# Causal masks of attention from TensorE to VectorE, and softmax maxima from matmuls to DMA, in a fused scan, attention and experts kernel

## The reference, cut to what matters

```python
t = t + attn(ln_t(t), Wk, Wq, Wv, Wu, bu)     # t: 8 images x 1024 tokens x 128
# inside attn, 8 heads of 128:
dot = einsum('bhqe,bhke->bhqk', queries, keys) / sqrt(e)
dot = where(tril(ones(t, t)), dot, -inf)
attn = softmax(dot, axis=-1)
out = einsum('bhqk,bhke->bqhe', attn, values).reshape(b, t, h * e)
return out @ Wu.T + bu
```

## Time and profile before

| | |
|---|---|
| median of 3 runs | 2596.7 us (2596.37 to 2597.08) |
| profiled execution, its own time | 2594.88 us |
| its span, first to last instruction | 2593.1 us |
| PE busy | 2389.7 us (92%) |
| DVE busy | 1641.9 us (63%) |
| POOL busy | 1636.7 us (63%) |
| ACT busy | 1359.5 us (52%) |
| mean granted TensorE clock | 0.921 |

### The profile page before, as it was taken

One profiled execution on the slowest core, in us unless ns is written; L12 is line 12 of the kernel. 1 busy time (PEld: TensorE's weight loads), 2 busy tenths in 40 slices (PEclk: granted clock), 3 DMA queues, 4 the chain that ended last, 5 costly groups with the idle time before them and its releaser, 6 DMA issues. The chain is left out here.

```text
span 2593.1 us, 45062 instructions
## 1 busy us (share of the span) xinstructions
PE 2389.7 (92%) x14307; PEld 1954.7 (75%) x14307; DVE 1641.9 (63%) x3626; ACT 1359.5 (52%) x3319; POOL 1636.7 (63%) x1773
## 2 busy tenths in 40 slices
PE   4798999999996999999999999999999999399994
PEld 2577777777774888888888888888888887288883
DVE  5777877787545566666666666667666664244444
ACT  3655565655532566666566656665666655133331
POOL 3678877887741556576676675766756758255551
PEclk9987887887786999999999999999999999599996
DMA  3920000000000000010010010100100100255555
GB/s 103 386 97 2 9 9 1 9 1 1 17 1 25 1 1 23 2 32 9 3 36 3 8 33 2 33 8 4 36 2 9 33 1 32 79 195 194 196 187 196
DMA packets 61693, 130.97 MB, mean 51 GB/s; under 512 B 9157, under 2 KB 27631, under 8 KB 61462
## 3 DMA queue, kind: packets, MB, share of 16 engines
q1 hardware_dynamic: 51222, 106.82, 12.1%
q0 software_dynamic: 9088, 17.07, 1.9%
q10 hardware_dynamic: 1152, 4.19, 0.4%
HBM read 64.78 MB, written 65.10 MB: 50 GB/s over the span
## 5 line engine op out<-in xcount | busy, mean ns | idle before, releaser
L1135 POOL TENSOR_TENSOR plo<-pf,phi 128x512 fp32r<-128x512 f32 (+3 forms) x768 | 775.8, 1014 | 478.4 <-ACT phi L1374 403.7
L1372 ACT ACTIVATE pf<-psum 128x512 f32<-128x512 f32 (+3 forms) x768 | 378.0, 492 | 498.0 <-PE psum L1274 343.9
L1515 DVE TENSOR_REDUCE peak<-psum 128x1 f32<-128x512 f32 (+3 forms) x512 | 302.9, 592 | 229.2 <-PE psum L1245 121.6
L1374 ACT ACTIVATE phi<-psum 128x512 fp32r<-128x512 f32 (+3 forms) x768 | 374.5, 488 | 0.0
L1245 PE MATMUL psum<-xT,qT 128*128 128x512 f32 (+3 forms) x768 | 304.1, 396 | 10.8 <-DVE nmax L1509 5.2
L1194 PE MATMUL psum<-phi,x_tok 128*128 128x512 f32 (+3 forms) x768 | 307.5, 400 | 0.0
L1194 PE MATMUL psum<-qT,xT 128*128 128x512 f32 (+3 forms) x768 | 266.8, 347 | 0.0
L1196 PE MATMUL psum<-phi,x_tok 128*128 128x512 f32 (+3 forms) x768 | 265.9, 346 | 0.0
L1196 PE MATMUL psum<-qT,xT 128*128 128x512 f32 (+3 forms) x768 | 265.7, 346 | 0.0
L1195 PE MATMUL psum<-qT,xT 128*128 128x512 f32 (+3 forms) x768 | 265.0, 345 | 0.0
L1195 PE MATMUL psum<-plo,x_tok 128*128 128x512 f32 (+3 forms) x768 | 264.7, 345 | 0.0
(11 more groups left out here) (275 smaller groups left out, 5642.2 us busy)
## 6 DMA issues: line engine op xcount, KB each, us to landing
wg<-turned_w SPq DMA_DIRECT2D x39, 874.0 KB
routed<-empty SPq DMA_DIRECT2D x1, 34056.0 KB, 96.7
xg<-routed SPq DMA_DIRECT2D x39, 264.0 KB
y<-chosen SPq DMA_DIRECT2D x8, 1024.0 KB, 10.3
turned_w<-wT SPq DMA_DIRECT2D x8, 874.0 KB, 4.4
x_in_sb<-in_x SPq DMA_DIRECT2D x8, 512.0 KB, 3.8
out<-o_st ACTq DMA_DIRECT2D x8, 512.0 KB, 5.7
chosen<-yg,xg POOLq DMA_INDIRECT x156
```

What stands on the lines that cost most here:

```text
L1135: g_.tensor_tensor(plo[:, T % RP, 0:n], pf[:, T % RP, 0:n], phi[:, T % RP, 0:n].bitcast(F32), ALU.subtract).then_inc(a["low_ready"], 1)
L1372: s_.activation(pf[:, T % RP, 0:n], bank[T % RS][:, 0:n], ACT.Exp)
L1374: s_.activation(phi[:, T % RP, 0:n], bank[T % RS][:, 0:n], ACT.Exp).then_inc(a["high_ready"], 1)
L1515: v.reduce_max(peak[:, g % 2, m_:m_ + 1], bank[3][:, 0:n], AX, negate=True).then_inc(a["peak_found"], 1)
```

## The change

TensorE no longer adds masks. find_peak of a diagonal piece becomes one fused instruction on VectorE, which adds a 512-wide mask from SBUF (ahead_wide, zeros and then mask_ahead), writes the sum to a scratch tile (masked) and takes the maximum. mask_diag, a new VectorE instruction before find_peak, adds mask_after to the 128 columns of a diagonal score piece in PSUM, and the exponentials of such a piece wait for it.

The maxima are no longer negated; instead row 0 of xT holds -1.0, and the weights that read that row (vu_w's last column and the bias row) change sign. peak_row and set_row are gone. SP moves each tile's 128 maxima, one number from each partition, into qT's row 0 by a DMA, four DMAs a half, eight a head. SP's list is then, for each head, the two moves, and behind those of every eighth head the store of one expert's turned weights and the load of the next.

```diff
-                    g_.memset(xnt[:, :, 0:1], 1.0).then_inc(s["pad_zero"], 1)
+                    g_.memset(xnt[:, :, 0:1], -1.0).then_inc(s["pad_zero"], 1)
...
-                if p == 1 and is_head(g):
-                    yield "row", g, 1
...
-                if p == 6 and is_head(g + 1):
-                    yield "row", g + 1, 0
...
+                    def move_row(g, half):
+                        sp.wait_ge(a["peak_joined"], 2 * g + half + 1)
+                        sp.wait_ge(a["q_ready"], 2 * g + half + 1)
+                        with nc.allow_non_contiguous_dma("a column of each partition to one row"):
+                            for j in range(NH1):
+                                q0 = half * HALF + j * P
+                                sp.dma_start(qT[0:1, g % 2, 0, q0:q0 + P].bitcast(F32),
+                                             nmax[:, g % 2, half * NH1 + j:half * NH1 + j + 1].bitcast(F32)).then_inc(row_set[half], 16)
...
+                    for g in range(NG_):
+                        for half in range(2):
+                            move_row(g, half)
+                        if g % NH == 0:
+                            if g:
+                                store_weights(g // NH - 1)
+                            load_weights(g // NH)
+                    store_weights(E - 1)
...
-                        last = t.matmul(bank[3][:, 0:n], qT[:, g % 2, 0, i * P:(i + 1) * P], xT[:, b % 2, 0, k0:k0 + n],
-                                        start=True, stop=not diag)
-                        if diag:
-                            last = t.matmul(bank[3][:, n - P:n], ident_bf[:, :], mask_ahead[:, :], start=False, stop=True)
-                        last.then_inc(a["peak_ready"], 1)
-
-                    def peak_row(g, half):
...
+                        t.matmul(bank[3][:, 0:n], qT[:, g % 2, 0, i * P:(i + 1) * P], xT[:, b % 2, 0, k0:k0 + n],
+                                 start=True, stop=True).then_inc(a["peak_ready"], 1)
...
-                            pe.wait_ge(a["row_set"], 2 * g + half + 1)
+                            pe.wait_ge(row_set[half], 16 * NH1 * (g + 1))
...
-                        if diag:
-                            last = t.matmul(to[:, 0:P], ident_bf[:, :], mask_after[:, :], start=False, stop=True)
-                        last.then_inc(a["scores_ready"], 1)
...
                         act.wait_ge(a["scores_ready"], T + 1)
+                        if is_diag(T):
+                            act.wait_ge(a["diag_masked"], diags_before(T) + 1)
...
-                    v.tensor_copy(vu_w[:, :, P:P + 1], ident[:, 0:1].unsqueeze(1).to_broadcast([P, NH, 1]))
-                    v.tensor_copy(ident_r[:, :], ident[:, :])
+                    v.tensor_scalar(vu_w[:, :, P:P + 1], ident[:, 0:1].unsqueeze(1).to_broadcast([P, NH, 1]), -1.0, None, ALU.mult)
+                    v.memset(ahead_wide[:, 0:HALF - P], 0.0)
+                    v.tensor_copy(ahead_wide[:, HALF - P:HALF], mask_ahead[:, :]).then_inc(a["wide_made"], 1)
...
+                        if diag:
+                            need2(dve, "peak_found", g * NP + m_)
+                            v.tensor_tensor_reduce(out=masked[:, 0:n], in0=bank[3][:, 0:n], in1=ahead_wide[:, HALF - n:HALF], scale=1.0,
+                                                   scalar=NEG, op0=ALU.add, op1=ALU.max, accum_out=to).then_inc(a["peak_found"], 1)
+                        else:
+                            v.reduce_max(to, bank[3][:, 0:n], AX).then_inc(a["peak_found"], 1)
...
+                    def mask_diag(T):
+                        dve.wait_ge(a["scores_ready"], T + 1)
+                        v.tensor_tensor(bank[T % RS][:, 0:P], bank[T % RS][:, 0:P], mask_after[:, :], ALU.add).then_inc(a["diag_masked"], 1)
...
-                    def set_row(g, half):
...
+                        if is_head(g) and is_diag(T):
+                            mask_diag(T)
                         if is_head(g + 1):
                             find_peak(g + 1, p)
```

More of the change, by code:

```diff
@@ L1068, in image_after, with is_diag, diags_before @@
                 return b if g % NH == h and 0 <= b < B else None
+            def is_diag(T):
+                half, kt, q0, n = PIECES[T % NP]
+                return kt >= NH1 * half
+            def diags_before(T):
+                return NC * (T // NP) + sum(1 for p in range(T % NP) if is_diag(p))
             def u_count(g, half):
@@ L1244, in peak_scores @@
                         need2(pe, "peak_found", g * NP + m_)
-                        last = t.matmul(bank[3][:, 0:n], qT[:, g % 2, 0, i * P:(i + 1) * P], xT[:, b % 2, 0, k0:k0 + n],
-                                        start=True, stop=not diag)
-                        if diag:
-                            last = t.matmul(bank[3][:, n - P:n], ident_bf[:, :], mask_ahead[:, :], start=False, stop=True)
-                        last.then_inc(a["peak_ready"], 1)
-                    def peak_row(g, half):
[L1252 to L1255, removed]
-                            last = t.matmul(to[0:1, j * P:(j + 1) * P], nmax[:, g % 2, i:i + 1], ident_r[:, :],
-                                            start=True, stop=True)
-                        last.then_inc(a["row_ready"], 1)
+                        t.matmul(bank[3][:, 0:n], qT[:, g % 2, 0, i * P:(i + 1) * P], xT[:, b % 2, 0, k0:k0 + n],
+                                 start=True, stop=True).then_inc(a["peak_ready"], 1)
                     def scores(T):
@@ L1267, in scores @@
                             pe.wait_ge(a["q_ready"], 2 * g + half + 1)
-                            pe.wait_ge(a["row_set"], 2 * g + half + 1)
+                            pe.wait_ge(row_set[half], 16 * NH1 * (g + 1))
                         cols = slice(half * HALF + q0, half * HALF + q0 + n)
-                        diag = kt >= NH1 * half
-                        last = mm3(to[:, 0:n], [xT[:, b % 2, k, kt * P:(kt + 1) * P] for k in range(2)],
-                                   [qT[:, g % 2, k, cols] for k in range(2)], True, not diag)
-                        if diag:
-                            last = t.matmul(to[:, 0:P], ident_bf[:, :], mask_after[:, :], start=False, stop=True)
-                        last.then_inc(a["scores_ready"], 1)
+                        mm3(to[:, 0:n], [xT[:, b % 2, k, kt * P:(kt + 1) * P] for k in range(2)],
+                            [qT[:, g % 2, k, cols] for k in range(2)], True, True).then_inc(a["scores_ready"], 1)
                     def attend(T):
@@ L1344, in _ @@
                                 tokens(*which)
-                            elif kind == "row":
-                                peak_row(*which)
                             elif kind == "queries":
@@ new lines, in find_peak @@
+                            to = nmax[:, g % 2, i:i + 1]
+                        else:
+                            to = peak[:, g % 2, m_:m_ + 1]
+                        if diag:
[4 more added lines that the diff above has]
+                            v.reduce_max(to, bank[3][:, 0:n], AX).then_inc(a["peak_found"], 1)
@@ L1707, in _ @@
                             add_output(g - 1, 1, p - 4)
-                        if p == 6 and is_head(g + 1):
-                            set_row(g + 1, 0)
                         if p in (8, 10) and is_head(g):
```

37 lines of the change are left out of this document (17 added, 20 removed).

## The result

The changed kernel takes 2530.2 us in the median of four runs (2525.6 to 2533.6), the kernel before 2596.9 (2596.4 to 2597.1): ratio 0.974, 95% interval 0.9725 to 0.9759. The forecast was 2536. The profiled execution is the fastest of the four, 2525.6 us with a span of 2523.6.

The account below looks back on a forecast made before the run. Attention was taken as bound by TensorE's instruction stream: -2.33 + 0.65 + 0.6 + 0.1 = -1.0 us a head, -63 us, and +2 once, about -61 from 2596.7, so 2536 us; range 2465 to 2625.

Parts of the forecast that it names:

- Rival C: VectorE's fused add and maximum runs at half rate; stalls of 2.9 us a head against 2.33, 2630 us; chance 0.15.
- Rival D: The row lands late by DMA; TensorE waits 0.3 to 1.8 us at scores(4), 2555 to 2650 us; chance 0.13.
- The sum: Attention, per head: TensorE's saving, VectorE's stalls, routing and the row's DMA make -1.0 us, -63 us in all.
- The first term: TensorE sheds 16 masks at 0.115 us (1.85) and the row matmuls (0.48): 2.33 us a head, 149 us.
- the walk: Step-by-step timing of VectorE and TensorE through a head from p = 9: four peak-bank stalls, 0.65 us a head in all.
- 0.65 + 0.6: Given back on VectorE per head: 0.65 us of peak-bank stalls, 0.6 us of routing and next-image input work.
- the row waits: TensorE's wait at scores(4) for the row's DMA: 0 to 1.3 us a head, 0.1 taken on average.
- low_query's: VectorE's low_query waits for ScalarE's high_query at p = 9 and 2, behind exponentials that now wait for VectorE's mask.
- the routing pieces: VectorE's routing and next-image inputs: hidden at p = 3 and 7, half showing at p = 11 and 0, 0.6 us a head.

Follow-up runs that it names:

- no_mask_matmuls: The kernel before with its 16 mask matmuls a head left out and nothing in their place, so attention is not causal: 2495.8 us, ratio 0.9609.
- no_score_mask: The changed kernel without mask_diag only, the fused pass kept: 2491.2 us, ratio 0.9587 to the kernel before.
- rows_in_eight: The changed kernel with each DMA of a row cut in two, 16 issues a head instead of 8: 2600.1 us, ratio 1.001 to the kernel before.
- no_masks_at_all: The changed kernel without mask_diag and with plain maxima in place of the fused pass: 2482.5 us, ratio 0.9556 to the kernel before.
- routing_moved: The changed kernel with six pieces of VectorE's routing and input work moved from p = 11 and 0 to p = 4 to 7: 2558.6 us, ratio 0.9851.
- tensor_masks_0_1: The changed kernel with the score masks of p = 0 and 1 alone added by TensorE again: 2541.5 us, ratio 0.9792 to the kernel before.
- late_query: The changed kernel with VectorE's low_query one step later, p = 3 and 10 in place of 2 and 9: 2551.0 us, ratio 0.9821.

## Why the prediction was right

**Right in mechanism.** TensorE's stream was the bound and each matmul taken out is time gained; VectorE's fixed order gives a part back through the one peak bank; the rows land in time. no_mask_matmuls, no_score_mask and rows_in_eight show each of the three by itself. Rival C (the fused pass at half rate) is out by its own row, 0.681 us for 512 columns. For the Trainium skill's pitfall in the Vector Engine (DVE) Microarchitecture Reference, half the throughput with two non-bf16 SBUF sources, this was a pass with one of the two in PSUM, and it ran at full rate. Rival D (late rows) did not happen, and rows_in_eight shows how far off it was: 1.3 us on average, 0.5 us at h = 0.

**Wrong in size, twice, in opposite directions.** The sum read -2.33 + 0.65 + 0.6 + 0.1 us a head. The first term is 102 + 24 us over 64 heads, 1.97: the mask was priced at 0.115 us and is 0.099, since beside peak matmuls of 128 or 256 columns it is worth 0.07 to 0.08; the rows were priced at 0.48 and gave 0.38, since the bank that find_peak(6) frees holds peak(7) once they are gone, a stall that the walk had at nothing. By the isolated gap in the Trainium skill (TensorE: Matmul & The Clock Gate, Back-to-back issue gap) the whole term would be 86 us against 126 measured, so the trace was the better guide, if not exact. The prediction took the lower of two figures: the same section of the Trainium skill says that the isolated one under-counts at few columns and gives 81 ns as the sustained spacing at 128, by which the masks alone are estimated at 83 us, against 102 measured. What VectorE gives back is 11 + 8 + 40 = 59 us, 0.92 a head, where the prediction had 0.65 + 0.6 = 1.25: the undisturbed head stalls by 0.3 in place of 0.65, the rest adds 0.5 to 0.6. The accumulator's read is recorded with 0.083 us (0.1 taken) and the mask with 0.293 (0.30 taken), but in the queue they take nearly nothing and 0.197; the row waits 0.05 us a head (0.1 taken). The net is 1.97 - 0.92 = 1.05 us against 1.0, and the agreement within 6 us is partly luck: the errors of 23 us and 21 us, plus some 6 for the rows' waits, nearly cancelled.

**The step that failed.** The walk held one kind of forced wait, low_query's, and priced all else on VectorE as pieces of work. Two things it did not hold. First, low_tokens at h = 6 and low_weights at h = 7 stand at p = 0 and wait for ScalarE in the same way, behind exponentials that now wait for a mask. Against no_masks_at_all, the distance from peak(1) to peak(2) grew there by 1.1 and 0.6 us, 0.2 us a head over all eight. VectorE's line at h = 6:

```profile
1270.58 0.69 DVE L1508 TENSOR_TENSOR x_tok<-psum,x_tok 128x512 fp32r<-128x512 f32 x1 [1.50 <-ACT x_tok L1434]
```

Second, a VectorE pass can be held up by one of GpSimd's. The prediction said that at p = 3 and 7 VectorE's idle time still takes the routing pieces, and that from p = 4 to 8 it is idle again. Six pieces moved to p = 4 to 7 cost 28 us (routing_moved), and their records there show such meetings.

**Left open.** How much of the 0.5 us that the other heads lose comes from their work and how much from meetings with GpSimd was not separated by a run. The records speak for work and order in the changed kernel itself: ten kinds of its routing and input pieces take 93.1 us in all behind 830 us, 92.4 in no_masks_at_all and 92.3 in the kernel before, so they were not held up longer in sum. And the eight small instructions at p = 11 of h = 4, behind which peak(1) of h = 5 is late by 0.65 us, have their usual lengths. tensor_masks_0_1 fits the second reading by its rows, but no run removed GpSimd's passes.

## What to carry to other kernels

When work leaves the engine that bounds a stage, price it by the distance between starts with and without it, in several neighbourhoods, not by its length nor in one place. An in-order engine that receives work is judged by the waits in its fixed order and by how far it may lag, here one bank, so one step; a wait in that order may stand in time that is free, and taking it away can cost more than it gave (late_query). Lengths mislead on VectorE as they do on TensorE: price what is added there by starts too. Measure the room of a transfer that seems hidden by making it later, and read it head by head: here 2.4 us more on a hidden DMA cost the whole gain of the change.

## What the runs showed of the hardware that was not expected

A VectorE instruction with SBUF operands can wait for GpSimd inside its own recorded duration. The clearest case is the 4.36 us above for a 512-element subtraction with both inputs in SBUF, beside GpSimd passes of which three follow each other without a gap. The same kind of wait sits in the kernel before and is gone in the changed one, at one place (groups by form, 1000 to 2000 us, first before, then after):

```profile
L1621 DVE TENSOR_TENSOR both<-first,second 128x64 bf16<-128x64 f32 x6 | 7.9, 1317 | 0.2
```

```profile
L1639 DVE TENSOR_TENSOR both<-first,second 128x64 bf16<-128x64 f32 x6 | 1.3, 224 | 0.2
```

The same addition of 64 elements took 1317 ns before and 224 after, with nothing done to it: its moment fell beside GpSimd's pass (1.29 us for 512 elements) in one kernel and not in the other. The ends show that it is a wait for that pass. The choice of the first expert (`first<-pick,counted`, 64 elements) starts 0.38 us into a pass in the kernel before and 0.46 us into one in the changed kernel; it takes 0.98 and 0.94 us, and ends 0.08 us after the pass in all fourteen cases. In the one image of each trace in which no pass runs beside it, it takes 0.225. The choice of the second, which has started 0.21 us before a pass does, is not held up: 0.224. The join of the maxima, once in each head, takes 0.163 us alone and 0.274 beside the end of a pass in the kernel before, and 0.45 in most heads of the changed one:

```profile
1515.40 0.46 POOL L1162 TENSOR_TENSOR plo<-pf,phi 128x128 fp32r<-128x128 f32 x1 [0.57 <-ACT phi L1385]
```

This pass starts 0.03 us before the join at 1515.43 shown above, and both end within 0.02 us of each other. The Trainium skill (SBUF — State Buffer, Who interferes with whom and Summary: rules for kernel authors) says that a VectorE instruction with two SBUF inputs contends with a GpSimd instruction that reads SBUF, and that the second to issue is blocked until the first is through; these traces agree, and show the blocked one kept out through three passes in a row (the 4.36 us). In tensor_masks_0_1 the choice of the second expert (`second<-pick,counted`, 64 elements, in the head h = 4) took 1228 ns on average where the changed kernel takes 224: shifts of a few tenths of a microsecond decide such meetings. So versions of this schedule can differ by some 10 us for no reason in their own work (h = 4 lost 2.0 us there, some 15 over all images), and small reorderings here could not be forecast from VectorE's and TensorE's rows alone.
